# Attention maxima of two heads at a time on the two row halves of TensorE

## The chip, the cores and the metric

The kernel runs on one core of a Trainium2 chip. The time is the device time of one execution in microseconds (us), the median of three. The engines are PE (TensorE), DVE (VectorE), ACT (ScalarE), POOL (GpSimd) and SP (SyncE, which issues the transfers).

## The reference, cut to what matters

Four layers work on x of 4 batches x 512 positions x 128. Layers 0 and 2 are a selective scan and an attention with a triangular solve; the change does not touch them. Layers 1 and 3 are the same function, an attention of 16 heads of 8 columns and a choice among 8 experts:

```python
scores = jnp.einsum('bhqd,bhkd->bhqk', q, k) / jnp.sqrt(jnp.float32(D))
attn = jax.nn.softmax(scores, axis=-1)
o = jnp.einsum('bhqk,bhkd->bhqd', attn, v)
x = x + (o.transpose(0, 2, 1, 3).reshape(b, s, h) @ wo + bo)
# layer norm, logits, argmax over 8 experts, relu(h w1 + b1) w2 + b2 of the chosen expert
```

## The kernel before

`ffn_phase` (from L945) writes the program of layers 1 and 3, layer 1 at about 301 to 616 us of the span and layer 3 in its last 300 us. A float32 q and k are each split into three bf16 parts. A product of a head is taken as one bf16 matmul with 72 contracted rows, all nine pairs of parts by 8 columns. Each head is worked twice. First the maxima: for each of the 4 tiles of 128 queries a matmul of 72 rows against 512 keys into one PSUM bank (`for_maximum`, L1811), and a DVE reduction of that bank to the negated row maximum (`maximum`, L1480). Then the scores: a matmul with keys as rows, with 75 contracted rows of which three carry the maxima (`score`, L1830), the exponential on ACT (`exponential`, L1361), and, once for four scores, eight float32 matmuls with 32 output columns each that weight the values (`weighted`, L1841).

A batch has 64 such steps (16 heads x 4 tiles), numbered mu = 0 to 63 in batch m; a loop over i = 64 m + mu writes the program of each engine in order. In step i PE issues the maximum of step i, then the score of step i - 32. Where mu leaves 2 when divided by 4, `weighted` follows the score. Below, four steps that begin at a multiple of 4 are a group of four. Other work of PE is placed at fixed mu: turned maxima at 2, 18, 34, 51; outputs turned (L1780) at 7, 22, 38, 55; and, at 0, 13, 25, 28, 31, 42, 45, 48, 60, the routing logits and ranks of the batch two before, the norms, projections and values of the next batch, and the output projection and second norm of the last one. DVE follows the same step order, with `shift_split` (five small operations, L1489 to L1497) after the maximum of mu 0, 16, 32, 48, and with norms and divisions between.

Maxima share three PSUM banks, scores three others:

```python
if n >= MAX_BANKS:
    pe.wait_ge(s["max_out"], n - MAX_BANKS + 1)
```

So the matmul of maximum n waits for the reduction of maximum n - 3. Operands of even batches lie in `first_ops`, of odd ones in `second_ops`; SP loads them for the next batch from DRAM, where the parts are stored, in four groups of four heads (`load_group`), each one query transfer of 288 KB and three key transfers of 96 KB. In the same queue stand `shifts` (12 KB of maxima into the operands, four a batch) and `load_walls` (expert weights, 578 KB each, two at a time behind batches 1, 2 and 3, and two at the end). Layer 3 is entered with half of batch 0's maxima already made.

Of the kernel before, what the change touches and what calls it, by code (L numbers as in the profile page):

```python
# [15 lines left out]
BF16 = mybir.dt.bfloat16  # L16
# [4 lines left out]
P = 128  # L21
B, S, H = 4, 512, 128
# [859 lines left out]
PARTS = 3  # L882
# [21 lines left out]
def query_rows(scr):  # L904

    return scr.rearrange("i d h s -> (i d) h s").unsqueeze(1).to_broadcast([PARTS * HD, PARTS, scr.shape[2], S]).rearrange(
        "r j h s -> r j (h s)")
# [9 lines left out]
    return scr.rearrange("d j h s -> (d j) h s")  # L917


def rows_of_part(i):  # L920
    return slice(i * PARTS * HD, (i + 1) * PARTS * HD)

# [8 lines left out]
AT_SPLIT_MAXIMA = (16, 32, 48, 64)  # L931
AT_TURN_GROUP = (55, 71, 86, 102)
STEPS = GROUPS * TPB
SCORE_BANKS = 3
MAX_BANKS = 3
STAGES = 3
# [8 lines left out]
def ffn_phase(core, nc, tag, stores=False, entered=False):  # L945
# [4 lines left out]
    with ExitStack() as ctx:  # L950
# [110 lines left out]
        def unit(b, u):  # L1061
            return b * UNITS + u - skipped_units
# [5 lines left out]
            return 16 * (b + 1 - (k < skipped_quarters))  # L1068

        def operand_loads(b, g):  # L1070
            loads = (1 + PARTS) * (b // 2 + 1)
            if b % 2 == 0:
                loads -= 1 + PARTS if entered or g < KEY_GROUPS else 1
            return 16 * loads

        def prepared_at(m):
            return (None, None, None) if m + 1 < split_early else (25, 28, 31)
# [79 lines left out]
        with nc.Block() as block:  # L1157
# [98 lines left out]
            def _(sp):  # L1256
# [7 lines left out]
                def load_group(b, g):  # L1264
                    if b >= 2:
                        sp.wait_ge(s["s_ps"], (b - 2) * UNITS + (g + 1) * GROUP * TPB)
                    heads = slice(g * GROUP, (g + 1) * GROUP)
                    sp.dma_start(q_op(b, slice(0, QK_ROWS))[:, heads, :], query_rows(q_scr[stored(b), :, :, heads, :])).then_inc(
                        op_in[b % 2][g], 16)
                    load_keys(b, g, heads)  # L1270
# [11 lines left out]
                def load_walls(first):  # L1282
                    for e in range(first, first + E // 4):
# [11 lines left out]
                for b in range(B):  # L1295
                    for k in range(QUARTERS // 2):
                        if b > 0 or k >= skipped_quarters:
                            shifts(b, k)
                    if skipped < b + 1 < B:
                        store_parts(b + 1)  # L1300
                        for g in range(GROUPS // 2):
                            load_group(b + 1, g)
                    shifts(b, 2)
                    if skipped < b + 1 < B:
# [153 lines left out]
            def _(dve):  # L1458
# [18 lines left out]

                def maximum(b, u):
                    dve.wait_ge(s["max_ps"], unit(b, u) + 1)
                    nc.vector.tensor_reduce(row_min[:, b % 2, u // TPB, u % TPB:u % TPB + 1], ps[:, MAXQ[unit(b, u) % MAX_BANKS], :],  # L1480
                                            AX.X, ALU.max, negate=True).then_inc(s["max_out"], 1)

                def shift_split(b, k):
# [293 lines left out]
            def _(pe):  # L1777
# [25 lines left out]
                    last.then_inc(s["v_ps"], 1)  # L1803

                def for_maximum(b, u):
                    hd, t, n = u // TPB, u % TPB, unit(b, u)
                    if u % (GROUP * TPB) == 0 and operand_loads(b, hd // GROUP):
                        pe.wait_ge(op_in[b % 2][hd // GROUP], operand_loads(b, hd // GROUP))
                    if n >= MAX_BANKS:
                        pe.wait_ge(s["max_out"], n - MAX_BANKS + 1)  # L1810
                    nc.tensor.matmul(ps[:, MAXQ[n % MAX_BANKS], :], q_op(b, QK)[:, hd, t * P:(t + 1) * P],  # L1811
                                     k_op(b, QK)[:, hd, :], start=True, stop=True).then_inc(s["max_ps"], 1)

                def turn_maxima(b, k):
                    pe.wait_ge(s["m_split"], SPLIT_OPS * (quarter(b, k) + 1))
# [1406 lines left out]
```

## Time and profile before

| | |
|---|---|
| median of 3 runs | 1382.33 us (1380.26 to 1384.09) |
| the profiled execution, its own time | 1384.38 us |
| its span, first to last instruction | 1382.3 us |
| PE busy | 1162.0 us (84%) |
| DVE busy | 982.6 us (71%) |
| ACT busy | 686.8 us (50%) |
| mean granted clock of PE | 0.901 of 2.4 GHz |

Times in the trace are us from the span's start. An end of a matmul is modelled: a following one starts before it, so distances between starts are what counts on PE. "PEld" is the load of a matmul's weights, "SPq" an issue of a transfer.

### The profile page before, as it was taken

The page shows a single profiled execution, that of the slowest core. Times are in us where ns is not written, and L with a number is a line of the kernel's source. Part 1 is how long each engine was busy: PE and PEld are TensorE (multiplying, and loading weights), DVE is VectorE, ACT ScalarE, POOL GpSimd, SP SyncE. Part 2 cuts the span into 40 slices and gives each one's busy share as a digit, 9 for nine tenths or more (in the row PEclk, how much of TensorE's full clock was granted, in tenths as well). Part 3 has the DMA queues.
Part 4 walks back from the last instruction along what each step waited for, and adds up shares of the span by engine and source line. Part 5 has one row for each costly group of instructions (what it writes and reads, how often), then busy time and mean ns, then how long its engine had stood idle before and what let it go on. Part 6 is the DMA issues. An engine that isn't in the chain of part 4 may idle for free. (4 is left out here: it accounts for less than half of the span.)

```text
span 1382.3 us, 33189 instructions
## 1 busy us (share of the span) xinstructions
PE 1162.0 (84%) x12998; PEld 630.4 (46%) x13034; DVE 982.6 (71%) x2128; ACT 686.8 (50%) x1425; POOL 619.0 (45%) x828
## 2 busy tenths in 40 slices
PE   6846668768999998797887888988989999999875
PEld 2212333323333334774465666666666433333375
DVE  5699999988888884545775674645735688888453
ACT  3844344414776767441362352442441377776754
POOL 2359889965234321541452353352442243432153
PEclk9968989997999999898899888979988799999988
DMA  4387934231231402227133223223132303140223
GB/s 149 123 297 298 350 154 180 79 79 35 60 93 51 120 9 87 60 75 136 25 70 68 47 46 89 31 62 74 33 81 49 72 2 93 48 123 10 87 59 90
DMA packets 132800, 127.65 MB, mean 92 GB/s; under 512 B 86295, under 2 KB 117847, under 8 KB 128122
## 3 DMA queue, kind: packets, MB, share of 16 engines
q1 hardware_dynamic: 124592, 117.65, 30.0%
q0 software_dynamic: 2496, 5.13, 1.2%
q10 hardware_dynamic: 5558, 2.76, 0.9%
q8 instruction: 103, 1.69, 0.5%
q14 instruction: 51, 0.42, 0.1%
HBM read 104.83 MB, written 37.90 MB: 103 GB/s over the span
## 5 line engine op out<-in xcount | busy, mean ns | idle before, releaser
L1480 DVE TENSOR_REDUCE f_row_min<-f_ps 128x1 f32<-128x512 f32 x480 | 308.1, 682 | 54.5 <-PE f_ps L1811 53.8
L1361 ACT ACTIVATE f_e<-f_ps 128x512 f32<-128x512 f32 x512 | 279.2, 598 | 124.6 <-PE f_ps L1830 123.8
L816 PE MATMUL m_ps<-m_shared,sb_ident 128*128 128x512 f32 x256 | 134.1, 671 | 55.2 <-DVE m_shared L664 53.1
L379 POOL TENSOR_TENSOR m_drive<-m_du,m_ring 128x1024 f32<-128x1024 f32 x64 | 149.6, 2351 | 51.0 <-DVE m_ps L656 32.2
L522 ACT ACTIVATE m_ps<-m_delta,m_A 128x511 f32<-128x511 f32 x128 | 82.9, 681 | 118.7 <-DVE m_ps L656 98.2
L1841 PE MATMUL f_ps<-f_e,f_v_op 128*32 128x512 f32 x1024 | 137.3, 608 | 2.4 <-ACT f_e L1361 1.4
L2701 DVE TENSOR_REDUCE d_row_min<-d_ps 128x1 f32<-128x384 f32 (+3 forms) x176 | 104.6, 632 | 26.4 <-PE d_ps L2936 25.3
L816 PEld LDWEIGHTS m_ps<-m_shared,sb_ident 128*128 128x128 f32 x256 | 51.5, 212 | 139.8 <-DVE m_shared L664 81.8
L656 DVE TENSOR_TENSOR_SCAN m_ps<-m_ps,m_drive 128x1024 f32<-128x1024 f32 x44 | 101.1, 2297 | 5.0
L1811 PE MATMUL f_ps<-f_second_ops 72*128 72x512 bf16 x256 | 98.0, 383 | 2.8 <-DVE f_row_min L1480 2.8
L1830 PE MATMUL f_ps<-first_ops 75*128 75x512 bf16 x256 | 99.5, 389 | 0.0
L1811 PE MATMUL f_ps<-first_ops 72*128 72x512 bf16 x224 | 92.3, 421 | 8.4 <-DVE f_row_min L1480 6.2
L1830 PE MATMUL f_ps<-f_second_ops 75*128 75x512 bf16 x256 | 92.2, 381 | 2.6 <-ACT f_e L1361 2.6
L2933 PE MATMUL d_ps<-first_ops 96*128 96x128 bf16 (+3 forms) x256 | 67.3, 328 | 14.5 <-DVE d_row_min L2701 6.7
L3099 PE MATMUL d_ps<-d_mT,d_a_hop 16*32 16x16 f32 (+3 forms) x3584 | 68.9, 210 | 12.3 <-DVE d_a_hop L2858 8.1
L2344 POOL TENSOR_TENSOR d_prod<-d_xT_blk 128x14 f32<-128x14 f32 (+6 forms) x224 | 63.0, 281 | 17.5
L2349 POOL TENSOR_TENSOR d_xT_blk<-d_xT_blk,d_prod 128x14 f32<-128x14 f32 (+6 forms) x224 | 62.1, 277 | 17.5
L1215 POOL DMA_INDIRECT f_rows_scr<-f_h2n,f_place_u x32 | 31.8, 992 | 82.7 <-DVE f_place_u L1598 75.1
L3099 PEld LDWEIGHTS d_ps<-d_mT,d_a_hop 16*32 16x32 f32 (+1 forms) x3584 | 53.3, 117 | 31.1 <-issue 16.2
L1399 ACT ACTIVATE first_ops<-f_ps,first_ops 128x128 f32<-128x128 f32 x184 | 52.6, 369 | 27.3 <-PE f_ps L1897 27.3
L2338 POOL TENSOR_TENSOR d_xT_blk<-d_e_blk,d_zi_blk 128x256 f32<-128x256 f32 x16 | 14.4, 899 | 115.5 <-DVE d_zi_blk L2773 110.0
L2544 ACT ACTIVATE d_e_off<-d_ps 128x384 f32<-128x384 f32 (+1 forms) x112 | 55.7, 552 | 17.1 <-PE d_ps L2970 16.9
(319 smaller groups left out, 2297.5 us busy)
## 6 DMA issues: line engine op xcount, KB each, us to landing
m_ring<-bc_scr SPq DMA_DIRECT2D x32, 1024.0 KB, 5.4
f_rows_scr<-blank SPq DMA_DIRECT2D x2, 8707.5 KB, 31.0
f_wall<-f_wall SPq DMA_DIRECT2D x16, 578.0 KB, 5.1
first_ops<-q_scr SPq DMA_DIRECT2D x28, 288.0 KB
first_ops<-k_scr SPq DMA_DIRECT2D x84, 96.0 KB
f_second_ops<-q_scr SPq DMA_DIRECT2D x16, 288.0 KB
f_second_ops<-k_scr SPq DMA_DIRECT2D x48, 96.0 KB
f_second_ops<-f_rows_scr SPq DMA_DIRECT2D x36, 64.5 KB, 1.8
```

The costliest lines, as they stand in the source:

```text
L379: nc.gpsimd.tensor_tensor(drive[:, step % AHEAD, :].rearrange("p (a s) -> p a s", a=HALVES), du[:, :, tokens(b)], b_row(step).unsqueeze(1) ...
L522: last = nc.scalar.activation(ps[:, at + 1:at + S], delta[:, k, b * S + 1:(b + 1) * S], ACT.Exp, scale=A[:, k, n:n + 1])
L656: nc.vector.tensor_tensor_scan(h, bank(DECAY + HALVES * (step % 2), HALVES), drive[:, step % AHEAD, :], 0.0, ALU.mult, ALU.add).then_inc(s ...
L816: last = nc.tensor.matmul(bank(Y + k), core.ident[:, :], hC[:, k * S:(k + 1) * S], start=False, stop=last_of_batch)
L1361: nc.scalar.activation(e_sb[:, n % 3, hh, :], ps[:, SCORE[(b * UNITS + u) % SCORE_BANKS], :], ACT.Exp, scale=SCALE).then_inc(s["e_out"], 1)
L1480: nc.vector.tensor_reduce(row_min[:, b % 2, u // TPB, u % TPB:u % TPB + 1], ps[:, MAXQ[unit(b, u) % MAX_BANKS], :], AX.X, ALU.max, negate= ...
L1811: nc.tensor.matmul(ps[:, MAXQ[n % MAX_BANKS], :], q_op(b, QK)[:, hd, t * P:(t + 1) * P], k_op(b, QK)[:, hd, :], start=True, stop=True).the ...
L1830: nc.tensor.matmul(ps[:, SCORE[n % SCORE_BANKS], :], k_op(b, QKS)[:, hd, t * P:(t + 1) * P], q_op(b, QKS)[:, hd, :], start=True, stop=True ...
L1841: last = nc.tensor.matmul(ps[hh * HEAD_COLS:(hh + 1) * HEAD_COLS, O_BANK, :], v_of(b, t, g * GROUP + hh), e_sb[:, n % 3, hh, :], start=(t ...
L2701: nc.vector.tensor_reduce(row_min[:, n % 2, g * heads:(g + 1) * heads], dve_bank("maximum", n, g)[:, 0:heads * cols].rearrange("p (h c) -> ...
L2933: nc.tensor.matmul(bank[:, hh * cols:(hh + 1) * cols], q_op[0:SHIFT_AT, hd, rows_of(t)], k_op[0:SHIFT_AT, hd, 0:cols], start=(hh == 0), st ...
L3099: last = nc.tensor.matmul(ps[q * SPAN:(q + 1) * SPAN, STEP[n % 2], r * SPAN + cols.start:r * SPAN + cols.stop], a_hop[own, g * SPAN:(g + 1 ...
```

## The change

In batches 1 to 3 the maxima of two heads of a group are made as a pair of matmuls of 64 rows, one head from partitions 0 to 63, the other from partitions 64 to 127. For the second kind, half of the heads are also copied to partitions 64 to 127 of a tile that lies on the first four expert weights (`high_ops`). The last 8 of the 72 rows (third part of q by third part of k) are left out of these maxima; the rows of both operands are put in another order so that they come last. The scores keep all rows. The order of PE changes in all batches: at an even step both maxima of the pair are issued, then the score of that step, and at the odd step only its score.

The order in which heads are worked within a group for the maxima changes with `unit_at`; DVE writes each maximum to the place of its head. A group of heads now takes eight transfers of 832 KB together, 416 for each of q and k (192 + 96 + 96 + 32), instead of 576 KB. Groups 1 to 3 stand later in SP's queue. A load also waits for the maxima of the batch before, since `high_ops` is there once and not per batch parity. Weights 4 to 7 are loaded behind batches 1 and 2, weights 0 to 3 after the last maximum.

```diff
+        high_ops = wall[HALF:P, 0:SHARED_WALLS, :].rearrange("p e c -> p (e c)").bitcast(BF16)[:, 0:2 * (NH // 2) * S].rearrange(
+            "p (i h s) -> p i h s", i=2, s=S)
...
+        def unit_at(b, u):
+
+            if b == 0:
+                return u // TPB, u % TPB, 0
+            g, v = divmod(u, GROUP * TPB)
+            a, v = divmod(v, 2 * TPB)
+            return g * GROUP + v % 2 * IN_HALF + a, v // 2, v % 2
...
                 def load_group(b, g):
                     if b >= 2:
                         sp.wait_ge(s["s_ps"], (b - 2) * UNITS + (g + 1) * GROUP * TPB)
+                        sp.wait_ge(s["max_ps"], unit(b - 1, (g + 1) * GROUP * TPB))
...
+                        low, rest = of_rows(scr[stored(b), :, :, heads, :])
+                        sp.dma_start(rows[0:LOW_ROWS, heads, :], low).then_inc(op_in[b % 2][g], 16)
+                        sp.dma_start(rows[LOW_ROWS:QK_ROWS, heads, :], rest).then_inc(op_in[b % 2][g], 16)
+                        low, rest = of_rows(scr[stored(b), :, :, high_heads, :])
+                        sp.dma_start(high_ops[0:LOW_ROWS, i, in_high, :], low).then_inc(op_in[b % 2][g], 16)
+                        sp.dma_start(high_ops[LOW_ROWS:HALF, i, in_high, :], rest[0:PARTS - 1]).then_inc(op_in[b % 2][g], 16)
...
                         store_parts(b + 1)
-                        for g in range(GROUPS // 2):
-                            load_group(b + 1, g)
+                        load_group(b + 1, 0)
                     shifts(b, 2)
-                    if skipped < b + 1 < B:
-                        for g in range(GROUPS // 2, GROUPS):
-                            load_group(b + 1, g)
+                    if goes_on:
+                        load_group(b + 1, 1)
+                        load_group(b + 1, 2)
                     shifts(b, 3)
-                    if b >= 1:
-                        load_walls((b - 1) * E // 4)
-
-                load_walls(3 * E // 4)
+                    if goes_on:
+                        load_group(b + 1, 3)
+                    if b in (1, 2):
+                        load_walls(range(SHARED_WALLS + (b - 1) * E // 4, SHARED_WALLS + b * E // 4))
+
+                sp.wait_ge(s["max_ps"], unit(B, 0))
+                load_walls(range(SHARED_WALLS))
...
                 def for_maximum(b, u):
-                    hd, t, n = u // TPB, u % TPB, unit(b, u)
+                    hd, t, half = unit_at(b, u)
+                    n = unit(b, u)
...
-                    nc.tensor.matmul(ps[:, MAXQ[n % MAX_BANKS], :], q_op(b, QK)[:, hd, t * P:(t + 1) * P],
-                                     k_op(b, QK)[:, hd, :], start=True, stop=True).then_inc(s["max_ps"], 1)
+                    if half:
+                        slot = hd // GROUP * IN_HALF + hd % IN_HALF
+                        q_rows, k_rows = high_ops[:, 0, slot, :], high_ops[:, 1, slot, :]
+                    else:
+                        rows = QK if b == 0 else slice(0, HALF)
+                        q_rows, k_rows = q_op(b, rows)[:, hd, :], k_op(b, rows)[:, hd, :]
+                    nc.tensor.matmul(ps[:, MAXQ[n % MAX_BANKS], :], q_rows[:, t * P:(t + 1) * P], k_rows,
+                                     start=True, stop=True).then_inc(s["max_ps"], 1)
...
-                    if m < B:
+                    if m < B and mu % 2 == 0:
                         for_maximum(m, mu)
+                        for_maximum(m, mu + 1)
                     if 0 <= b < B:
                         score(b, u)
```

## Rows read from the trace of the kernel before

**Rows 1.** The page: busy time, share and instructions by engine

```profile
PE 1162.0 (84%) x12998; PEld 630.4 (46%) x13034; DVE 982.6 (71%) x2128; ACT 686.8 (50%) x1425; POOL 619.0 (45%) x828
```

**Rows 2.** Stretches of batches 1, 2, 3: length, busy PE, PEld, DVE, ACT, POOL, clock, DMA

```profile
353.50:409.89 56.39, 54.65 (x310) 19.18 (x308) 47.45 (x113) 40.11 (x78) 20.73 (x20) 1.00 0.29 69
409.89:467.77 57.88, 55.65 (x331) 20.76 (x330) 49.06 (x125) 40.24 (x78) 27.30 (x26) 1.00 0.29 81
467.77:521.90 54.13, 52.33 (x315) 18.48 (x314) 47.45 (x114) 37.51 (x74) 9.38 (x10) 1.00 0.10 31
1115.05:1171.43 56.38, 54.64 (x310) 19.20 (x309) 47.43 (x113) 40.13 (x78) 20.73 (x20) 1.00 0.23 55
```

**Rows 3.** Waits, 353.5 to 521.9: us in total, times, longest

```profile
ACT f_e L1361 <- PE f_ps L1830: 51.0, 73, 1.7
...
PEld f_ps L1811 <- DVE f_row_min L1480: 37.5, 73, 1.0
...
DVE f_row_min L1480 <- PE f_ps L1811: 22.0, 47, 1.0
```

**Rows 4.** Timeline of batch 1, mu 8 to 12: start, duration

```profile
359.96 0.38 PE L1811 MATMUL f_ps<-f_second_ops 72*128 72x512 bf16 x1
...
360.18 0.38 PE L1830 MATMUL f_ps<-first_ops 75*128 75x512 bf16 x1
...
360.38 0.69 DVE L1480 TENSOR_REDUCE f_row_min<-f_ps 128x1 f32<-128x512 f32 x1 [0.18 <-PE f_ps L1811]
360.40 0.38 PE L1811 MATMUL f_ps<-f_second_ops 72*128 72x512 bf16 x1
...
361.05 0.38 PE L1830 MATMUL f_ps<-first_ops 75*128 75x512 bf16 x1
...
361.36 1.06 PE L1841 MATMUL f_ps<-f_e,f_v_op 128*32 128x512 f32 x8
...
362.36 0.39 PE L1811 MATMUL f_ps<-f_second_ops 72*128 72x512 bf16 x1
...
362.66 0.68 DVE L1480 TENSOR_REDUCE f_row_min<-f_ps 128x1 f32<-128x512 f32 x1
...
363.40 0.10 PEld L1811 LDWEIGHTS f_ps<-f_second_ops 72*128 72x128 bf16 x1 [0.49 <-DVE f_row_min L1480]
```

**Rows 5.** Timeline of layer 0, matmuls of 128 and of 64 rows

```profile
46.66 1.01 PE L763 MATMUL m_ps<-m_shared,sb_m_dt 64*128 64x512 f32 x2
47.61 0.70 PE L745 MATMUL m_ps<-m_shared,sb_m_W 128*128 128x512 f32 x1
...
47.09 0.59 PE L763 MATMUL m_ps<-m_shared,sb_m_dt 64*128 64x512 f32 x1
...
53.70 0.59 PE L745 MATMUL m_ps<-m_shared,sb_m_W 128*128 128x512 f32 x1
54.22 0.69 PE L763 MATMUL m_ps<-m_shared,sb_m_dt 64*128 64x512 f32 x1
```

**Rows 6.** Timeline of batch 2, ranks: short matmuls in a row

```profile
420.92 0.17 PE L1880 MATMUL f_ps<-f_onehot_b,sb_all_before 128*128 128x8 bf16 x1
420.95 0.17 PE L1880 MATMUL f_ps<-f_onehot_b,sb_before 128*128 128x8 bf16 x1
```

**Rows 7.** Timeline of batch 1, mu 16 to 24, around a split

```profile
366.54 0.38 PE L1811 MATMUL f_ps<-f_second_ops 72*128 72x512 bf16 x1
...
373.09 0.38 PE L1811 MATMUL f_ps<-f_second_ops 72*128 72x512 bf16 x1
...
368.69 1.88 DVE L1480 TENSOR_REDUCE f_row_min<-f_ps 128x1 f32<-128x512 f32 x3
```

**Rows 8.** SP's issues for batch 1, and stretches behind them (columns as Rows 2)

```profile
342.19 0.87 SPq L1268 DMA_DIRECT2D f_second_ops<-q_scr  x1
...
356.00:358.00 2.00, 2.00 (x9) 0.54 (x8) 2.00 (x4) 1.28 (x4) 0.00 (x0) 1.00 0.69 145
358.00:360.00 2.00, 2.00 (x16) 0.88 (x16) 1.77 (x4) 1.67 (x4) 0.00 (x0) 1.00 0.12 33
```

More of the change, by code:

```diff
@@ L917, in key_rows, with ordered_query_rows, ordered_key_rows @@
     return scr.rearrange("d j h s -> (d j) h s")
+def ordered_query_rows(scr):
+    low, high, heads = scr[0:PARTS - 1], scr[PARTS - 1], scr.shape[2]
+    return (low.rearrange("i d h s -> (i d) h s").unsqueeze(1).to_broadcast([(PARTS - 1) * HD, PARTS, heads, S]).rearrange(
+        "r j h s -> r j (h s)"),
+        high.unsqueeze(0).to_broadcast([PARTS, HD, heads, S]).rearrange("j d h s -> j d (h s)"))
+def ordered_key_rows(scr):
+    heads = scr.shape[2]
+    return (scr.rearrange("d j h s -> (d j) h s").unsqueeze(0).to_broadcast([PARTS - 1, PARTS * HD, heads, S]).rearrange(
+        "i r h s -> i r (h s)"), scr.rearrange("d j h s -> j d (h s)"))
 def rows_of_part(i):
@@ L933 @@
 STEPS = GROUPS * TPB
+HALF = P // 2
+LOW_ROWS = (PARTS - 1) * PARTS * HD
+IN_HALF = GROUP // 2
+GROUP_LOADS = 8
+SHARED_WALLS = E // 2
 SCORE_BANKS = 3
@@ L1070, in operand_loads @@
         def operand_loads(b, g):
[L1071 to L1074, printed above, removed]
+            first = 0 if b % 2 or entered or g < KEY_GROUPS else PARTS
+            return 16 * (first + GROUP_LOADS * ((b + 1) // 2))
+        def unit_at(b, u):
[4 more added lines that the diff above has]
+            return g * GROUP + v % 2 * IN_HALF + a, v // 2, v % 2
         def prepared_at(m):
@@ L1266, in load_group @@
                         sp.wait_ge(s["s_ps"], (b - 2) * UNITS + (g + 1) * GROUP * TPB)
[L1267 to L1270, printed above, removed]
+                        sp.wait_ge(s["max_ps"], unit(b - 1, (g + 1) * GROUP * TPB))
+                    heads, in_high = slice(g * GROUP, (g + 1) * GROUP), slice(g * IN_HALF, (g + 1) * IN_HALF)
+                    high_heads = slice(g * GROUP + IN_HALF, (g + 1) * GROUP)
+                    for i, rows, of_rows, scr in ((0, q_op(b, slice(0, QK_ROWS)), ordered_query_rows, q_scr),
+                                                  (1, k_op(b, slice(0, QK_ROWS)), ordered_key_rows, k_scr)):
+                        low, rest = of_rows(scr[stored(b), :, :, heads, :])
[4 more added lines that the diff above has]
+                        sp.dma_start(high_ops[LOW_ROWS:HALF, i, in_high, :], rest[0:PARTS - 1]).then_inc(op_in[b % 2][g], 16)
                 def load_keys(b, g, heads):
@@ L1280, in shifts, with load_walls @@
                                  max_part[:, k, :]).then_inc(m_in[k], 16)
-                def load_walls(first):
-                    for e in range(first, first + E // 4):
+                def load_walls(experts):
+                    for e in experts:
                         sp.dma_start(wall[:, e, :], core.dram["f_wall"][:, e, :]).then_inc(s["wall_in"], 16)
@@ L1298, in _ @@
                             shifts(b, k)
-                    if skipped < b + 1 < B:
+                    goes_on = skipped < b + 1 < B
+                    if goes_on:
                         store_parts(b + 1)
-                        for g in range(GROUPS // 2):
-                            load_group(b + 1, g)
+                        load_group(b + 1, 0)
                     shifts(b, 2)
-                    if skipped < b + 1 < B:
-                        for g in range(GROUPS // 2, GROUPS):
-                            load_group(b + 1, g)
+                    if goes_on:
+                        load_group(b + 1, 1)
+                        load_group(b + 1, 2)
                     shifts(b, 3)
-                    if b >= 1:
-                        load_walls((b - 1) * E // 4)
-                load_walls(3 * E // 4)
+                    if goes_on:
+                        load_group(b + 1, 3)
[3 more added lines that the diff above has]
+                load_walls(range(SHARED_WALLS))
                 sp.wait_ge(s["rows_early_out"], 1)
@@ L1479, in maximum @@
                     dve.wait_ge(s["max_ps"], unit(b, u) + 1)
-                    nc.vector.tensor_reduce(row_min[:, b % 2, u // TPB, u % TPB:u % TPB + 1], ps[:, MAXQ[unit(b, u) % MAX_BANKS], :],
+                    hd, t, half = unit_at(b, u)
+                    nc.vector.tensor_reduce(row_min[:, b % 2, hd, t:t + 1], ps[:, MAXQ[unit(b, u) % MAX_BANKS], :],
                                             AX.X, ALU.max, negate=True).then_inc(s["max_out"], 1)
@@ L1805, in for_maximum @@
                 def for_maximum(b, u):
-                    hd, t, n = u // TPB, u % TPB, unit(b, u)
+                    hd, t, half = unit_at(b, u)
+                    n = unit(b, u)
                     if u % (GROUP * TPB) == 0 and operand_loads(b, hd // GROUP):
```

## The prediction

> **What bounds the kernel now.** I read the busy times first [rows 1]: PE is busy 84% of the span, more than any other engine, but that is a mean over four layers. So I cut out the stretches that the change touches, batches 1 to 3 of the two expert layers [rows 2]. There PE is busy 97% (54.65 of 56.39 us), DVE 84% (47.45), ACT 71%, and the granted clock is 1.00, its upper level of 2.4 GHz. One layer spends 56.39 + 57.88 + 54.13 = 168.4 us so, both 337 us. The waits [rows 3] say who is late: ACT waits 51.0 us for scores and has slack. DVE waits 22.0 us in 47 places for a maximum's matmul; the weight load of a maximum's matmul waits in 73 places for a reduction to free a bank. Most of those 37.5 us cost nothing, since a load waits while the matmuls before it still run, but the third bank back is never far.
>
> The timeline of a group of four without side work [rows 4] gives the units. Maximum to score is 0.22 us, score to maximum 0.22; the score before the weighting to its first matmul 0.31, and the eight weighting matmuls 1.00 until the next maximum starts. A group is 8 x 0.22 + 0.09 + 1.00 = 2.85 us, all of it PE. DVE starts a reduction 0.42 us after the matmul's start (359.96, 360.38), the reduction takes 0.68 to 0.69, and the weight load that waits for it starts 0.06 after its end (362.66 + 0.68 = 363.34, then 363.40).
>
> **The change, part by part.**
>
> *The pair's own matmuls.* If the halves work at once, one of two maxima disappears behind the other: -0.22 us a pair, -0.44 a group. How far apart do two start? No row has 64-row halves side by side. The lower bound is nothing; the nearest row is a row of full-height matmuls of 8 columns, each with its own weights, 0.03 us apart [rows 6]; the upper bound is no overlap, 0.22. I take 0.03.
>
> The page "TensorE: Matmul & The Clock Gate" of the Trainium skill (Part 3, the mechanism and the span model) puts tiles in different row groups about 4 ns apart; by it the group would be some 0.05 us shorter than with my 0.03, and no run here has shown it for row halves.
>
> *The change of tiling.* A 64-row matmul stands between 75-row scores. Layer 0 has both heights [rows 5]. Two 64-row matmuls in a row start 0.43 apart (46.66, 47.09); the one before a 128-row matmul is followed after 0.52 (47.09, 47.61), and 128 rows before 64 also after 0.52 (53.70, 54.22). So a change of height costs 0.09 us in each direction. The score before the 32-column weighting shows the same 0.09 (0.31 instead of 0.22) [rows 4]. These are float32 or column tiles; for bf16 halves I take 0.09 and keep 0 as the lower bound. A group has two pairs, each with one change in and one out: +4 x 0.09 = 0.36. Sum on PE: 2.85 - 0.44 + 2 x 0.03 + 0.36 = 2.83, a gain of 0.02 to 0.03. What row packing gives is taken by the changes of tiling.
>
> A rule of the Trainium skill speaks against this change, "TensorEngine Tiling (Array Packing)", Key Properties: a change of tiling mode drains the engine. The page gives no price; the trace agrees, with the 0.09 of layer 0. The same page's table under Theoretical Speedup gives up to 2x for a contraction of 64 or less; that is the first rival below.
>
> *The order of issue and the three banks.* This is what decides. The second matmul of a pair needs the reduction of the first one of the pair before. That is done 0.42 + 0.68 + 0.06 = 1.16 us after that matmul started. PE comes to it sooner where no weighting lies between, in the second pair of each group: 0.03 + 0.31 + 0.22 + 0.31 + 0.03 = 0.90. PE stands 0.26 us, with two scores and the weighting queued behind the wait. Across the weighting the distance is 1.9 us and nothing is waited for. So a bare group takes 2.83 + 0.26 = 3.09, 0.24 more than before. Before, the matching wait had four issues of 0.22 and the weighting to hide in, which is why 2.85 was all PE. If side work of PE lies between the pairs (at a mu that leaves 0 or 1 by 4, and it is 0.3 us or more), it hides the wait and the group gains 0.03. By the list of places that is mu 25, 28, 45, 48, 60 in batch 1, these and 0 and 13 in batch 2, and 0, 13, 45, 60 in batch 3. So of 48 groups 11 + 9 + 12 = 32 are bare and 16 covered.
>
> 32 x 0.24 = 7.7; 16 x -0.03 = -0.5. DVE's splits make part of this lighter: after the split at mu 16, the next reduction comes late, at 368.69, and the two groups of mu 16 to 23 took 373.09 - 366.54 = 6.55 us, with the turned maxima (0.17) and a turned output (0.44) and about 0.2 of waits that exist already [rows 7]. Carried through with the pair rule they take 6.8, +0.25 and not +0.48. The same holds for mu 32 to 39 and partly for 0 to 7, about -1.2 us over three batches. Batch 0 keeps full height but is issued in pairs too: the bank comes 1.16 after the first pair, PE after 5 x 0.22 = 1.10, 0.06 in some 8 groups, +0.5. Together 7.7 - 0.5 - 1.2 + 0.5 = 6.5 us a layer, 13 us for both.
>
> *The transfers.* A group of heads is 832 KB instead of 576, in eight issues instead of four. Before, the four groups of batch 1 (2304 KB) started at 342.19 and the engines were quiet from 358 on [rows 8], 144 KB a us. The new first group lands 832 / 144 = 5.8 us after 342.19, at 348, and is wanted at 353.5 [rows 2]. Groups 1 and 2 add 11.6 us and are done at about 360, the first of them wanted at 353.5 + 13. The maxima's `shifts` pass behind group 0 and behind groups 1 and 2: those of mu 51 follow at about 358 and are wanted 16 steps of 0.88 into batch 1, at 367. I cost it at nothing; if the cover were gone, some us per batch. The added wait for the batch before's maxima is past when each load is reached, since groups 1 and 2 follow the shifts of mu 51 (three fourths of the maxima) and group 3 those of the next batch's start. Nothing is queued behind it that is due sooner. Four experts' weights were loaded at the end before and are now, so the tail is as it was. DVE's and ACT's work is the same.
>
> *The eight products left out* change no time: in layer 0 matmuls of 64 and of 128 rows take the same 0.59 [rows 5].
>
> **How the sum stands.** The profiled execution took 1384.38 us with a span of 1382.3; the median is 1382.33. What is lost in batches 1 to 3 has no cover, since steps follow in order on PE. 1382.3 + 13 = 1395.
>
> **Rivals.**
>
> *Packing wins.* For: the engine that is busy 97% loses 0.44 us a group. It needs changes of tiling that cost nothing for bf16. Then covered groups gain 0.38, 16 x 0.38 = 6.1 us; bare ones are held by the bank: from first pair to second pair's end 1.16, then 0.22 + 0.31 + 1.00 + 0.22 = 2.91, +0.06, 1.9 us. Net -4, with batch 0 -3.7 a layer, -7: 1375. Without any bank wait it would be all 192 pairs x 0.22 = 42 us, 1340; the 1.16 excludes that. Against it are both rows at 0.52. Chance 0.08. It decides from a change of tiling under about 0.03.
>
> By the skill's Theoretical Speedup table alone the answer would be the 42 us.
>
> *The halves do not overlap.* Then the second starts 0.22 after the first. In bare groups 0.13 of it is not inside the bank wait, in covered ones 0.2 for both pairs each: 32 x 0.13 + 16 x 0.4 = 10.5 a layer, 21 more: 1416. For: no row shows two row tiles over all 128 columns at once. Against: the weighting's eight matmuls of 512 columns in 1.00 us overlap by columns. Chance 0.10.
>
> *Nothing moves.* The bank waits fall where PE waited anyway [rows 3], as in the groups with norms on DVE, and PE's and ACT's slack repays it: 1380 to 1386. Chance 0.12. Half of what is bare would have to be covered.
>
> *A transfer is late,* or DVE's side work adds to the pair's wait more than I let it: +20 to +30, 1402 to 1412. Chance 0.12.
>
> **How the numbers follow.** My case, a loss by the pair's bank wait, 1389 to 1402, has 0.58 and gives 1395. The range is 1378 to 1414: it takes in no change and nearly the rival without overlap. 0.3% (4 us) is what a measurement here can tell from no change. Faster has the 0.08 and 0.04 of the third rival, 0.12; same the rest of that and a little of my case's lower edge, 0.12; slower 0.76.
>
> **What would show it.** Maxima in pairs at most 0.03 apart; 0.31 from the second to the score, and from score to pair; the weight load of the second matmul in bare groups waiting for DVE, first pair to second pair's end 1.16, groups of mu 8 and 56 at 3.1 us. Stretches of about 58.5, 59.9 and 56.3 us. Distances of 0.22 at changes of height, or starts of pairs 0.22 apart, would prove me wrong, as would PE waiting for a transfer at mu 0, 16, 32 or 48.

## The result

| | before | changed |
|---|---|---|
| median | 1383.21 us (4 runs, 1380.26 to 1386.44) | 1462.47 us (4 runs, 1459.69 to 1474.66) |
| ratio | | 1.0597 (95%: 1.0556 to 1.0639) |
| profiled execution, its span | 1384.38, 1382.3 us | 1459.69, 1457.2 us |

The change costs about 79 us. The forecast was 1395 and its range ended at 1414, so the prediction is wrong: right in sign, and wrong by five sixths of the size. Where some runs of a kernel were longer than the rest at a lower clock from end to end, the times below are the median of the others.

### The profile page after: what moved, and what is told of

Read it like the earlier page. It is cut to its first block and busy times, and to the rows that moved or that the text cites. A ratio compares the mean times of both kernels' runs of the same rounds, so it can differ in the third digit from the quotient of the medians.

```text
span 1457.2 us, 33297 instructions
## 1 busy us (share of the span) xinstructions
PE 1190.6 (82%) x12998; PEld 613.4 (42%) x13034; DVE 983.6 (67%) x2128; ACT 697.6 (48%) x1425; POOL 618.3 (42%) x828
## 5 line engine op out<-in xcount | busy, mean ns | idle before, releaser
L1519 DVE TENSOR_REDUCE f_row_min<-f_ps 128x1 f32<-128x512 f32 x480 | 307.1, 681 | 120.2 <-PE f_ps L1857 119.4
L1399 ACT ACTIVATE f_e<-f_ps 128x512 f32<-128x512 f32 x512 | 288.9, 597 | 193.4 <-PE f_ps L1876 186.7
L816 PE MATMUL m_ps<-m_shared,sb_ident 128*128 128x512 f32 x256 | 133.3, 668 | 52.6 <-DVE m_shared L664 50.7
L1887 PE MATMUL f_ps<-f_e,f_v_op 128*32 128x512 f32 x1024 | 146.9, 647 | 2.1 <-ACT f_e L1399 1.4
L1876 PE MATMUL f_ps<-first_ops 75*128 75x512 bf16 x256 | 98.8, 423 | 32.8 <-DMA first_ops<-f_max_part 32.7
L1876 PE MATMUL f_ps<-f_second_ops 75*128 75x512 bf16 x256 | 88.6, 391 | 12.8 <-DMA f_second_ops<-f_max_part 10.2
L1857 PE MATMUL f_ps<-f_wall 64*128 64x512 bf16 x192 | 78.1, 407 | 2.3 <-DVE f_row_min L1519 1.8
L3146 PE MATMUL d_ps<-d_mT,d_a_hop 16*32 16x16 f32 (+3 forms) x3584 | 66.5, 206 | 15.6 <-DVE d_a_hop L2905 8.8
L2980 PE MATMUL d_ps<-first_ops 96*128 96x128 bf16 (+3 forms) x256 | 67.4, 327 | 13.3 <-DVE d_row_min L2748 6.3
L1857 PE MATMUL f_ps<-first_ops 72*128 72x512 bf16 (+1 forms) x160 | 66.1, 451 | 7.4 <-DVE f_row_min L1519 5.4
L1876 PEld LDWEIGHTS f_ps<-first_ops 75*128 75x128 bf16 x256 | 22.4, 100 | 103.6 <-ACT f_e L1399 40.7
```

What stands on the lines that cost most here:

```text
L816: last = nc.tensor.matmul(bank(Y + k), core.ident[:, :], hC[:, k * S:(k + 1) * S], start=False, stop=last_of_batch)
L1399: nc.scalar.activation(e_sb[:, n % 3, hh, :], ps[:, SCORE[(b * UNITS + u) % SCORE_BANKS], :], ACT.Exp, scale=SCALE).then_inc(s["e_out"], 1)
L1519: nc.vector.tensor_reduce(row_min[:, b % 2, hd, t:t + 1], ps[:, MAXQ[unit(b, u) % MAX_BANKS], :], AX.X, ALU.max, negate=True).then_inc(s[" ...
L1857: nc.tensor.matmul(ps[:, MAXQ[n % MAX_BANKS], :], q_rows[:, t * P:(t + 1) * P], k_rows, start=True, stop=True).then_inc(s["max_ps"], 1)
L1876: nc.tensor.matmul(ps[:, SCORE[n % SCORE_BANKS], :], k_op(b, QKS)[:, hd, t * P:(t + 1) * P], q_op(b, QKS)[:, hd, :], start=True, stop=True ...
L1887: last = nc.tensor.matmul(ps[hh * HEAD_COLS:(hh + 1) * HEAD_COLS, O_BANK, :], v_of(b, t, g * GROUP + hh), e_sb[:, n % 3, hh, :], start=(t ...
```

## The profile after

The page's busy times answer to [rows 1]. Lines have moved: the maxima's matmuls are at L1857, the scores at L1876, the weighting at L1887, the reductions at L1519. The loads of a group are issued at L1301 (low rows), L1302 (remaining rows), L1304 and L1305 (the same for the upper copies, in the tile `f_wall`), the shifts at L1314.

```profile
PE 1190.6 (82%) x12998; PEld 613.4 (42%) x13034; DVE 983.6 (67%) x2128; ACT 697.6 (48%) x1425; POOL 618.3 (42%) x828
```

PE is busy 28.6 us longer with the same number of instructions, and the span is 74.9 us longer. Both need a cause: idle time, and work that runs slower. The stretches of batches 1 to 3, first layer 1, then layer 3, with the columns of [rows 2]:

```profile
354.84:425.01 70.17, 64.93 (x308) 18.26 (x310) 48.14 (x112) 41.21 (x77) 20.70 (x20) 0.85 0.22 65
425.01:489.75 64.74, 59.25 (x331) 18.92 (x330) 49.20 (x124) 41.64 (x78) 27.26 (x26) 0.97 0.30 89
489.75:554.10 64.35, 57.27 (x306) 16.98 (x305) 46.37 (x112) 38.07 (x72) 9.36 (x10) 0.89 0.16 55
1147.51:1223.99 76.48, 59.62 (x310) 17.66 (x310) 47.86 (x112) 41.65 (x78) 20.70 (x20) 0.89 0.14 41
...
sum 408.35, PE 358.08 PEld 107.49 DVE 287.19 ACT 242.32 POOL 114.54; mean PE 59.68 PEld 17.92 DVE 47.87 ACT 40.39 POOL 19.09
```

Before, the same six stretches sum to 336.75 us, with PE busy 325.29, so 71.6 of the 74.9 us are in them. (A stretch ends at the last maximum of its batch. In a kernel in pairs a score and a weighting of the last group come after that, which the kernel before has done by then, x306 against x315 matmuls of PE in batch 3. So its stretches come out 1.4 us short a layer against those of the kernel before. From the first maximum of batch 1 to the last score of the layer, both layers together, it is 377.8 us before and 452.3 after, 74.5 more; differences to the kernel before that are named "to the last score" below are of this kind.) PE's idle time went from 11.5 to 50.3 us, and the granted clock, 1.00 before, is 0.85 to 0.97. The costliest groups name what ends the idle time; this is the last column:

```profile
L1876 PE MATMUL f_ps<-first_ops 75*128 75x512 bf16 x256 | 98.8, 423 | 32.8 <-DMA first_ops<-f_max_part 32.7
...
L1876 PE MATMUL f_ps<-f_second_ops 75*128 75x512 bf16 x256 | 88.6, 391 | 12.8 <-DMA f_second_ops<-f_max_part 10.2
```

The scores wait 42.9 us for the shifts, the 12 KB of maxima that become three rows of the operands. They wait for none of it before. The chain that ended last has 3% of the span in DMA and 4% in SP's issues. PE's timeline in batch 1 of each layer shows single waits:

```profile
354.84 0.39 PE L1857 MATMUL f_ps<-f_second_ops 64*128 64x512 bf16 x1 [2.34 <-DMA f_wall<-k_scr]
354.85 0.39 PE L1857 MATMUL f_ps<-f_wall 64*128 64x512 bf16 x1
...
377.03 1.03 PE L1876 MATMUL f_ps<-first_ops 75*128 75x512 bf16 x2 [3.70 <-DMA first_ops<-f_max_part]
378.00 0.60 PE L1857 MATMUL f_ps<-f_second_ops 64*128 64x512 bf16 x1
378.00 0.61 PE L1857 MATMUL f_ps<-f_wall 64*128 64x512 bf16 x1
378.54 0.61 PE L1876 MATMUL f_ps<-first_ops 75*128 75x512 bf16 x1
...
1163.30 1.03 PE L1876 MATMUL f_ps<-first_ops 75*128 75x512 bf16 x2 [15.40 <-DMA first_ops<-f_max_part]
```

The reader is to see two things beside the waits. The two halves of a pair start within 0.01 us (354.84 and 354.85): they do overlap. And after the wait a pair is 0.54 us ahead of the score that follows it (378.00, 378.54) where the full clock has 0.32. The two-microsecond stretches of the same time say why. Their last three columns are granted clock, DMA share and GB/s, as in [rows 8]:

```profile
344.00:346.00 2.00, 2.00 (x13) 0.43 (x12) 2.00 (x4) 1.74 (x5) 0.00 (x0) 1.00 0.27 95
358.00:360.00 2.00, 2.00 (x12) 0.32 (x4) 0.66 (x2) 0.17 (x1) 0.00 (x0) 0.50 0.17 66
360.00:362.00 2.00, 2.00 (x7) 0.34 (x5) 1.42 (x3) 2.00 (x5) 0.00 (x0) 0.50 0.13 51
374.00:376.00 2.00, 0.00 (x0) 0.00 (x0) 1.84 (x7) 0.00 (x0) 2.00 (x3) 1.00 0.19 66
...
378.00:380.00 2.00, 2.00 (x12) 0.40 (x11) 1.29 (x2) 1.42 (x3) 0.00 (x0) 0.50 0.13 51
```

The clock is 0.50, the lower level of 1.2 GHz, in stretches that follow an idle PE (the 2.34 us before 354.84, the 3.70 us before 377.03), and it is so after each of the other five waits for a shift too (4.30, 6.07, 15.40, 5.90 and 7.50 us). And the DMA share falls to 0.12 to 0.19, about 2/16 and 3/16 of the engines, in 14 of the 21 stretches from 344 to 386 us; between them it is 0.27 to 0.48. The last load of batch 1 is over at about 387, 46 us after the first issue at 340.83. Before, the share was 0.74 to 0.83 from 344 to 356 us, and the loads were over 16 us after the first issue [rows 8]. SP's issues of the same time:

```profile
340.83 0.59 SPq L1301 DMA_DIRECT2D f_second_ops<-q_scr  x1
...
345.62 0.61 SPq L1305 DMA_DIRECT2D f_wall<-k_scr  x1
346.27 0.76 SPq L1314 DMA_DIRECT2D first_ops<-f_max_part  x1
347.07 0.57 SPq L1301 DMA_DIRECT2D f_second_ops<-q_scr  x1
...
362.07 2.54 SPq L1305 DMA_DIRECT2D f_wall<-k_scr  x1
364.66 0.76 SPq L1314 DMA_DIRECT2D first_ops<-f_max_part  x1
```

This shift is issued in time, 364.66 for a use at about 373, and lands at 377. The one of the longest wait, in layer 3, is issued late as well: at 1151.38, when PE has stood for 3.5 us, since it stands behind issues of loads that take up to 3.09 us each, where those above take 0.6. From there it takes 11.9 us to land, as the chain shows:

```profile
1151.38 11.88 DMA first_ops<-f_max_part
```

## The experiments

The median of the kernel before beside e1 to e4 is 1382.8 us, beside e5 to e8 1388.5, and beside e9 1383.1. Whole times of different groups are compared by their distance to it. The sums of stretches are of one profiled execution each.

**The theory, shape:** a transfer is carried by no more engines than its outermost dimension has entries. Before, that dimension is 24 in all loads, the share 12/16 or a little more. Of the change's, it is 16 for the low rows of q, but 2 for those of k (`"i r h s -> i r (h s)"`: a copy index of 2 ahead of 24 rows), and 3, or 2 in the copies, for the remaining rows. If these all use the same engines (no view shows single engines), the busiest carries, per group, 96 + 48 of k and its copies' low rows, 32 + 16 of k's remaining rows, and 12 + 32 + 6 + 16 of q: 258 KB, where each of 12 engines carried 576 / 12 = 48. The loads end late, and the shifts stand behind them on the same engines. **Rivals:** the volume (832 instead of 576 KB) and its place in the queue are enough; or the pairing itself costs more than forecast.

**e1_spread: the same rows to the same places, in wide transfers.** Twelve a group instead of eight. Compute and bytes stay (one part of q has its rows in another order).

```diff
-GROUP_LOADS = 8
+GROUP_LOADS = 12
...
+                        load(to[0:LOW_ROWS], low.rearrange("i d h s -> (i d) h s").unsqueeze(1).to_broadcast(
+                            [LOW_ROWS // PARTS, PARTS, n, S]).rearrange("r j h s -> r j (h s)"))
+                        load(to[LOW_ROWS:HALF], high.unsqueeze(1).to_broadcast([HD, PARTS - 1, n, S]).rearrange("d j h s -> d j (h s)"))
+                        if hs is heads:
+                            load(to[HALF:QK_ROWS], high)
...
+                        for i in range(PARTS - 1):
+                            load(to[rows_of_part(i)], key_rows(parts))
+                        load(to[LOW_ROWS:HALF], parts[:, 0:PARTS - 1].rearrange("d j h s -> d j (h s)"))
+                        if hs is heads:
+                            load(to[HALF:QK_ROWS], parts[:, PARTS - 1])
```

> The change whole (pairs, halves, copies, SP's order), with the same 832 KB a group cut otherwise: every transfer's outermost dimension is now 8, 16 or 24 and no longer 2 or 3 (twelve transfers a group, row order of the third part of q by dimension instead of by part). Theory A: the 75 us come from transfers whose outermost dimension is 2 or 3 and which only 2 or 3 of the 16 DMA engines carry; this kernel then shows the pair's bank wait alone, +13 us, about 1396, no wait of PE for first_ops<-f_max_part, a granted clock of 1.00 in batches 1 to 3, and 3.13 us for a bare group as in the changed kernel. Rival B: the bytes (832 instead of 576 KB) and the number of issues are too many for the queue; then this kernel, with more issues, stays near 1460. Rival C: the 1.2 GHz clock of half-height pairs costs most; then 1430 or more with clocks under 0.95 in those stretches though no transfer is late.

Measured: 1403.08 us, ratio to the kernel before 1.0172 (1.009 to 1.0254). First the stretch of batch 1 in layer 1 and the sum of all six, then three stretches of 2 us during the loads:

```profile
351.61:410.75 59.14, 57.68 (x310) 17.66 (x310) 47.67 (x112) 41.62 (x78) 20.68 (x20) 1.00 0.28 82
...
sum 347.22, PE 339.29 PEld 106.82 DVE 285.81 ACT 242.25 POOL 114.42; mean PE 56.55 PEld 17.80 DVE 47.63 ACT 40.38 POOL 19.07
```

```profile
344.00:346.00 2.00, 2.00 (x16) 0.93 (x16) 1.19 (x2) 1.49 (x3) 0.00 (x0) 1.00 0.47 143
...
356.00:358.00 2.00, 2.00 (x13) 0.55 (x13) 1.82 (x4) 1.68 (x5) 0.00 (x0) 1.00 0.49 149
358.00:360.00 2.00, 2.00 (x12) 0.73 (x10) 1.09 (x4) 1.31 (x3) 0.00 (x0) 1.00 0.47 129
```

The same bytes, on more engines, and 61.1 us of the six stretches are gone (408.35 - 347.22; both kernels are in pairs, so their stretches end alike). 42.3 of them are idle time of PE (50.3 to 7.9), 18.8 are PE's busy time (358.08 to 339.29), which is the work at the lower clock: it is 1.00 throughout here, so pairs of half height do not bring the lower clock with them. The volume is not the cause. PE waits 0.5 us for shifts in all, instead of 42.9. What remains against before is 13.3 us to the last score (391.1 and 377.8), the pairing's own. The whole time is 7 us above the 1396 that was expected.

**e3_narrow: only the shapes.** The kernel before, its own 576 KB, its own order of PE, and the change's cut of the loads (4 transfers, outermost dimension 2 or 3 where the change has it). The diff is the change's two functions and:

```diff
-                    sp.dma_start(q_op(b, slice(0, QK_ROWS))[:, heads, :], query_rows(q_scr[stored(b), :, :, heads, :])).then_inc(
-                        op_in[b % 2][g], 16)
-                    load_keys(b, g, heads)
+                        low, rest = of_rows(scr[stored(b), :, :, heads, :])
+                        sp.dma_start(rows[0:LOW_ROWS, heads, :], low).then_inc(op_in[b % 2][g], 16)
+                        sp.dma_start(rows[LOW_ROWS:QK_ROWS, heads, :], rest).then_inc(op_in[b % 2][g], 16)
```

> The kernel before in its compute and in the place of its loads, 576 KB a group as before, but the loads cut as in the change: query rows 192 + 96 KB and key rows 192 + 96 KB, with outermost dimensions 16, 3, 2 and 3. Theory A: lowest engines carry 12 + 32 + 96 + 32 KB of each group instead of 48, a batch's loads last some 25 to 30 us instead of 16, shifts queued behind them come late, PE waits for first_ops<-f_max_part and f_second_ops<-f_max_part: 1400 to 1440. Rival B (bytes and issues): the same bytes and as many issues, 1383.

Measured, one run: 1421.29 us, the six stretches 384.86, 48 us over before without one pair of maxima. Two stretches of 2 us and one of the costliest groups:

```profile
356.00:358.00 2.00, 0.00 (x0) 0.00 (x0) 0.00 (x0) 0.00 (x0) 0.00 (x0) 0.50 0.19 68
362.00:364.00 2.00, 2.00 (x10) 0.22 (x10) 0.24 (x1) 0.57 (x1) 0.00 (x0) 0.50 0.13 53
```

```profile
L1848 PE MATMUL f_ps<-first_ops 75*128 75x512 bf16 x256 | 104.5, 408 | 16.7 <-DMA first_ops<-f_max_part 16.7
```

The shapes alone bring back the shares of 0.19 and 0.13, the waits for the shifts and the clock of 0.50. The whole time is inside the 1400 to 1440 expected. With e1 this is shown from both sides.

**e6_keys: which shape.** The changed kernel, with only the two key transfers of outermost dimension 2 (`low`, and the copies') each cut in two of 24 rows:

```diff
+                    def low_in(to, low, keys):
+                        for to, low in [(to[rows_of_part(p)], low[p]) for p in range(PARTS - 1)] if keys else [(to, low)]:
+                            sp.dma_start(to, low).then_inc(op_in[b % 2][g], 16)
```

> The changed kernel with one edit in its loads: the 48 key rows, until now one transfer with outermost dimension 2 (and another for the copies), go as two transfers of 24 rows; query rows and the rests keep their outermost dimension 2 or 3. Theory A by the load of the lowest DMA engine for a group: changed kernel 12 + 32 + 6 + 16 (queries) + 96 + 32 + 48 + 16 (keys) = 258 KB, here 12 + 32 + 6 + 16 + 16 + 32 + 8 + 16 = 138 KB, e1_spread 74 KB. A batch's four groups then need some 25 us and not 45: most waits for shifts go, 1400 to 1420. If width does not matter, two more issues a group make it 1460 or slower.

Measured, one run: 1398.91 us, stretches 350.14, no wait for the shifts. The two key transfers of outermost dimension 2, of a group's eight, carry almost the whole loss (58.2 of the 61.1 us). The whole time is just under the 1400 to 1420 expected. What the stretches stand above e1's, 2.9 us, isn't a late transfer: it lies in batch 2 of both layers (61.18 and 61.20 us against 59.62 and 59.64), where PE waits for no transfer and the clock is 0.50 for some 3 us at mu 12 with PE busy. Why it fell there is open.

```profile
L1881 PE MATMUL f_ps<-first_ops 75*128 75x512 bf16 x256 | 91.6, 393 | 0.0
```

**e7_shift_queue: who stands behind the loads.** The changed kernel, narrow loads and all, with the shifts issued from ACT's queue:

```diff
+                    act.wait_ge(s["m_out"], quarter(b, k) + 1)
+                    act.dma_start(q_op(b, slice(QK_ROWS, SHIFT_ROWS))[:, quarter_heads(k), :].rearrange("j h (t s) -> j (h t) s", t=TPB),
+                                  max_part[:, k, :]).then_inc(m_in[k], 16)
```

> The changed kernel with its narrow loads, but the 12 KB transfers of maxima (shifts) are issued by ACT on its own queue instead of SP's. Theory A: the shifts wait because they stand behind narrow loads in the same rings of the lowest engines; in rings of their own they get their turn between, PE's waits for f_max_part (some 43 us of idle PE) shrink to a few, PE waits now for loads at mu 0 and 16 if at all: 1405 to 1440. If the shifts are late since the engines themselves are overloaded, whatever the ring, 1450 or more.

Measured, one run: 1410.39 us, stretches 357.67, 50.7 less than the change. PE waits for no shift, and the whole time is inside the 1405 to 1440 expected. What stays is 10.5 us over e1. Of it 5.6 are in batch 1 of layer 1, which takes 64.72 at a mean clock of 0.89, after this wait for a load at its start:

```profile
355.74 0.39 PE L1858 MATMUL f_ps<-f_second_ops 64*128 64x512 bf16 x1 [2.13 <-DMA f_wall<-k_scr]
```

Another 2.5 are in batch 2 of layer 1, with a clock of 0.97 and no wait for a transfer. So most of the loss is the queue behind the narrow transfers, and a smaller part a load that itself comes late.

**e2_order: the pair's order alone.** The kernel before with the change's last hunk (both maxima at the even step), full height, no copies.

> The kernel before, with one edit: at an even step both maxima are issued, then the score; all maxima keep 72 rows, loads as before. Bank wait: the second pair's second matmul may start 1.16 us after the first pair's first, PE comes after 5 x 0.22 = 1.10, so 0.06 to 0.08 in bare groups, 48 x 0.07 = 3 us a layer at most: 1387 to 1391. If order alone does the harm of the change's pairs, 1396 or more; if it is free, 1383.

Measured: 1388.7 us, 1.005 (1.0005 to 1.0096), as expected; to the last score 4.8 us over before (382.6). A bare group of four is 2.93 (358.11 to 361.04), 0.08 more than in [rows 4]; the five issues of 0.22 from first pair to second pair's end cover 1.10 of the 1.17 that the bank takes.

**e4_same_half: both heads of a pair on the lower half.** e1 with `if False:` for `if half:` and without the copies' loads: no overlap, and 576 KB a group again; all else alike.

> As e1_spread, but both maxima of a pair come from partitions 0 to 63, so they cannot overlap, and the copies are not loaded (seven transfers a group, 576 KB). If halves overlap in the change, the second of the pair now starts 0.22 later: a group is 2.83 - 0.06 + 0.44 = 3.21 us with or without side work, +0.36 in 48 groups of each layer, 1415 to 1420, about 22 us over e1_spread. If halves do not overlap, it equals e1_spread.

Measured: 1408.46 us, 1.023 (1.0134 to 1.0327), stretches 360.08, 12.9 over e1. The whole times are 5.4 us apart, within their intervals. Bare groups take 3.25 (359.63 to 362.88), e1's 3.13, and the covered one of mu 28 4.97, e1's 4.55. The overlap is real, and in the stretches it is worth 12.9 us, not the 21 of the rival and the 22 expected. The rival counted each group as bare or covered. But mu 16 to 23 of batch 1 take 7.32 us in both kernels, and the group of mu 52 there takes 3.68 without the overlap and 4.06 with it; why it is slower with it is open.

**e5_banks: four banks for maxima, two for scores.** e1 with `MAX_BANKS = 4`, `SCORE_BANKS = 2`.

> e1_spread with one PSUM bank moved from the scores to the maxima: 4 and 2 instead of 3 and 3. Theory: the second matmul of a bare group's second pair (0.90 us after the first pair, bank back after 1.16) now waits for the reduction one place earlier and not at all; in exchange a score waits for the exponential of the second score before, which is done 0.42 + 0.60 = 1.02 us after that score's start. The second score of the second pair comes 0.31 + 0.03 + 0.31 + 0.22 = 0.87 after it, a wait of about 0.15. Bare groups go from 3.13 to between 2.85 and 3.05, batch 1 from 59.1 to about 57; the run 2 to 8 us under e1_spread. If the pair's wait is not the bank, bare groups stay at 3.13 or more.

Measured: 1419.55 us, 1.0214 (1.0156 to 1.0273), stretches 347.13, as e1. It was expected 2 to 8 us under e1 and came out over it. The second pair of a bare group:

```profile
359.84 0.39 PE L1868 MATMUL f_ps<-f_second_ops 64*128 64x512 bf16 x1
359.85 0.39 PE L1868 MATMUL f_ps<-f_wall 64*128 64x512 bf16 x1
...
360.44 0.39 PE L1887 MATMUL f_ps<-first_ops 75*128 75x512 bf16 x1 [0.21 <-ACT f_e L1410]
```

The pair is together again, so the bank was its wait. The score behind it now waits 0.21 us for the exponential to free one of two banks, and the group stays at 3.10. Outside the stretches the last scores of a layer, which run without maxima, take 34.9 us in layer 1, where the clock also is at 0.71 on average, and 27.8 in layer 3 at a clock of 1.00, instead of 23.4 in e1: 11.5 and 4.4 more, of the 22.6 that the profiled span is longer. The bank that the scores lack shows alone in the 4.4; how much of the 11.5 is the clock stays open. Moving a bank moves the wait.

**e8_height: the change of height alone.** The kernel before with 64-row maxima on the lower half in batches 1 to 3, one at a time as before.

```diff
+                    rows = QK if b == 0 else slice(0, P // 2)
+                    nc.tensor.matmul(ps[:, MAXQ[n % MAX_BANKS], :], q_op(b, rows)[:, hd, t * P:(t + 1) * P],
+                                     k_op(b, rows)[:, hd, :], start=True, stop=True).then_inc(s["max_ps"], 1)
```

> The kernel before with one edit: the matmuls of maxima of batches 1 to 3 contract 64 rows instead of 72 (the last 8 rows of the products are left out of the maxima alone), same order M S M S, same loads, no pairs. If a change of height between 64 and 75 rows costs 0.09 us each way, each step gains 0.18 us except where the weighting (a change anyway) stands: 7 changes more in a group, 0.63 us, 48 groups and two layers, partly inside other waits: +45 to +60 us, 1430 to 1443, bare groups 3.5 us instead of 2.85. If it costs nothing for bf16, 1383.

Measured: 1429.75 us, just under the 1430 to 1443 expected; stretches 389.50, 52.8 over before. PE in a bare group:

```profile
360.44 0.39 PE L1812 MATMUL f_ps<-f_second_ops 64*128 64x512 bf16 x1
360.76 0.39 PE L1831 MATMUL f_ps<-first_ops 75*128 75x512 bf16 x1
361.08 0.39 PE L1812 MATMUL f_ps<-f_second_ops 64*128 64x512 bf16 x1
361.40 0.39 PE L1831 MATMUL f_ps<-first_ops 75*128 75x512 bf16 x1
...
362.36 1.07 PE L1842 MATMUL f_ps<-f_e,f_v_op 128*32 128x512 f32 x8
...
364.00 0.39 PE L1812 MATMUL f_ps<-f_second_ops 64*128 64x512 bf16 x1
```

Every distance from 64 to 75 rows and from 75 to 64 is 0.32 instead of 0.22, and the group takes 3.56 instead of 2.85: 0.71 for seven changes, 0.10 each. The page "TensorEngine Tiling (Array Packing)" of the Trainium skill (Key Properties) says that a change of tiling mode drains the engine and gives no price; the trace agrees that it costs, and this is what it costs here. Two matmuls of 64 rows in a row (e4) start 0.22 apart, so it is the change and not the height.

**e9_after_score: the second pair one score later.** e1 with the second pair issued after the group's third score, ahead of the weighting, and batch 0 in its old order.

```diff
-                    if m < B and mu % 2 == 0:
+                    if m == 0:
+                        for_maximum(m, mu)
+                    elif m < B and mu % GROUP == 0:
                         for_maximum(m, mu)
                         for_maximum(m, mu + 1)
                     if 0 <= b < B:
                         score(b, u)
+                        if 1 <= m < B and mu % GROUP == 2:
+                            for_maximum(m, mu)
+                            for_maximum(m, mu + 1)
```

> e1_spread (wide loads, halves, copies) with another place of the second pair: after the third score of its group and right before the weighting, which is a change of tiling anyway; batch 0 has the order of the kernel before. By the two prices found so far: first pair, 0.34 to its score, three scores 0.66 in all, 0.31 to the second pair, whose second matmul finds its bank back at 1.16 (PE is there at 1.12), weighting 0.31 later, 1.00, the last score, 0.31 to the next pair: 2.78, by the 0.04 that e1_spread's groups stood over the same sum 2.82, instead of 3.13 there and 2.85 before. Batches 1 to 3 then take about what they took before (56.4, 57.9, 53.8 us) or 1 us less each, 1378 to 1386 in all. If the pair's wait is not about the distance of 1.16 us, groups stay near 3.1 and the run near 1397.

```profile
358.37 0.39 PE L1868 MATMUL f_ps<-f_second_ops 64*128 64x512 bf16 x1
358.37 0.39 PE L1868 MATMUL f_ps<-f_wall 64*128 64x512 bf16 x1
358.69 0.82 PE L1887 MATMUL f_ps<-first_ops 75*128 75x512 bf16 x3
359.44 0.39 PE L1868 MATMUL f_ps<-f_second_ops 64*128 64x512 bf16 x1
359.54 0.39 PE L1868 MATMUL f_ps<-f_wall 64*128 64x512 bf16 x1
359.86 1.07 PE L1898 MATMUL f_ps<-f_e,f_v_op 128*32 128x512 f32 x8
...
361.18 0.39 PE L1868 MATMUL f_ps<-f_second_ops 64*128 64x512 bf16 x1
```

The distance from first pair to second pair's end is again 1.17 (358.37 to 359.54), but three scores lie in it now and only 0.10 of it is waiting. The group is 2.81 us. To the last score it is 378.7 us, 0.9 over before, and 1.0 of it is one group, mu 12 of batch 1 in layer 1 (5.03 us, and 4.02 in batch 2), where the clock is 0.50 for 3.4 us without a wait for a transfer. The time is 1384.5 us, 1.0024 (0.9987 to 1.0061): no difference that can be measured. No version beats the kernel before.

## Why the prediction was wrong

**The step that failed is "The transfers", costed at nothing.** It divided 832 KB by 144 KB a us and let the first group land at 348. That rate is one of transfers whose outermost dimension is 24; it was carried over to eight transfers of which six have 2 or 3, and the DMA share beside it (0.69 in [rows 8], 0.74 to 0.83 just before) says with how many engines it was reached; it isn't a property of the queue. The new first group was there only at 354.84, the four took 46 us and not 23, and the shifts, said to "pass behind" the groups, came up to 15.4 us late. That step did name what is late next, and that the shifts are wanted at 367: with loads that last to 387 instead of 360 it would have found them late. Its "nothing is queued behind it that is due sooner" fails as well, since the shift issued at 364.66 stands behind loads that are due later. And its sign of being wrong, PE waiting for a transfer at mu 0 or 16, is what the trace shows, at 354.84 and 377.03. The rival "a transfer is late" had a chance of 0.12 and +20 to +30 us. By e1 it is 61.1 us in the stretches: two thirds idle time and one third the clock that is 0.50 after each of the seven waits, which was in no term at all. That the engines set the rate was readable: "DMA: Bandwidth & Descriptors" of the Trainium skill, section "Why a DMA increments its semaphore by 16 and not by 1", chooses the number of engines from the slowest dimension of both sides (the largest divisor up to 16), so 24 gives 12 and 2 gives 2, and its table row "Use all 16 engines" (Rules for kernel authors) warns of a leading broadcast dimension. The shares here, 0.74 to 0.83 for 24 (12/16 is 0.75; other transfers ran beside), 0.19 for 3 and 0.13 for 2, agree.

**The rest of the sum is near, in part by luck.** With the loads made wide (e1), the forecast can be compared term by term.

| | predicted | measured (e1, or as named) |
|---|---|---|
| two halves apart | 0.03 us | 0.00 to 0.01 |
| change of height, each way | 0.09 | 0.10 (e8) |
| first pair to second pair's end | 1.16 | 1.17 |
| bare group | 3.09 | 3.13 |
| covered group, mu 28 and 60 (changed kernel) | -0.03 | -0.02, -0.03 |
| mu 16 to 23 of batch 1 | +0.25 | +0.77 (7.32 for 6.55) |
| batches 1 to 3, both layers | 12 | 13.3 |
| batch 0, both layers | 1 | 2.3 |
| sum | 13 | 15.6 |

The bare group is 0.04 above the forecast, since a change of height costs 0.10, four a group. The sorting into bare and covered groups was too simple, and its errors cancel: against before, the group of mu 52 takes 0.44 more (4.06 and 3.62) and that of mu 12 in batch 1 0.29 more, while mu 24 and 48, forecast to gain 0.03, gain 0.18 and 0.20 (3.98 and 4.16, 3.90 and 4.10). Of mu 16 to 23 the forecast took +0.25 for each batch; batches 2 and 3 of layer 1 have -0.02 and -0.18. In batch 0 part of the 2.3 is a lower clock at its start, which lasts 27.3 us in e1's layer 1 and 23.9 before. The wait of the bare group stands in e1's timeline, in all engines' rows of batch 1:

```profile
358.48 0.39 PE L1868 MATMUL f_ps<-f_second_ops 64*128 64x512 bf16 x1
...
358.90 0.69 DVE L1530 TENSOR_REDUCE f_row_min<-f_ps 128x1 f32<-128x512 f32 x1 [1.08 <-PE f_ps L1868]
...
359.65 0.09 PEld L1868 LDWEIGHTS f_ps<-f_wall 64*128 64x128 bf16 x1 [0.22 <-DVE f_row_min L1530]
359.65 0.39 PE L1868 MATMUL f_ps<-f_wall 64*128 64x512 bf16 x1
```

0.42 to the reduction, 0.69 of it, 0.06 to the load of the weights. That e1's whole time stands 20 us above before and not 15.6 is not settled: from the last score of layer 1 to the first maximum of layer 3, where the program is the same, it is 543.9 us before, 547.3 in e1, and 536.6 (e9) to 554.3 (e5) in the others, and the interval of e1's ratio reaches down to 12 us. e6, whose stretches are 2.9 us longer than those of e1, stands only 10 above the kernel before in its one run.

**Rivals.** "Packing wins" needed free changes of height and falls with e8. "The halves do not overlap" falls with the 0.01 us and with e4. "Nothing moves" falls with e1, but e9 comes back to it: once the bank wait is gone, four changes of height eat what the overlap gives, 2.81 against 2.85.

## What to carry to other kernels

Before a transfer rate is carried over to a new transfer, compare their outermost dimensions: the DMA share of the profile shows how many engines carry it, and a short transfer that is due soon must not stand behind a narrow long one. Before matmuls are packed on row halves, count the changes of height and the free banks: here four changes of 0.10 us a group took 0.40 of the 0.44 that the overlap gives, and a pair that did not find two free banks waited. Waits of PE for transfers cost more than themselves here, because what followed each of the seven ran at the lower clock.

## What was not expected of the hardware

An engine of a narrow transfer moves more than one of a wide one: 51 GB/s at a share of 2/16 is 25 per engine, 66 at 3/16 is 22, and 158 at 0.74, some 12 engines, is 13. So the loss is smaller than the ratio of engines: 258 KB on the busiest engine instead of 48 is 5.4 times, and 46 us instead of 16 is 2.9. As an estimate from these numbers, four groups of 258 KB on one engine at 22 to 25 GB/s take 42 to 48 us, and 46 were measured, which fits all narrow transfers using the same few engines.

The clock of 0.50 lasts beyond the wait: it is 0.50 from 378 to 386 after the wait that ended at 377.03. The group of mu 4, with a turned output in it, takes 5.85 us at that clock in batch 1 (from 359.73) and 3.57 in e1. And it comes without such a wait too, as in e6 and e9 at mu 12.
